# A routed expert stage: 256-slot tiles against 64 full tiles and seven half tiles

## Time and profile before

| what | value |
|---|---|
| median of three runs | 830.58 us |
| the profiled execution's own time | 830.82 us |
| its span, first to last instruction | 829.0 us |
| instructions | 17062 |
| TensorE busy | 798.3 us, 96% |
| VectorE busy | 508.3 us, 61% |
| ScalarE busy | 372.2 us, 45% |
| GpSimd busy | 438.5 us, 53% |
| moved by DMA | 93.35 MB |

### The profile page before, as it was taken

One profiled execution on the slowest core, in us unless ns is written; L12 is line 12 of the kernel. 1 busy time (PEld: TensorE's weight loads), 2 busy tenths in 40 slices (PEclk: granted clock), 3 DMA queues, 4 the chain that ended last, 5 costly groups with the idle time before them and its releaser, 6 DMA issues.

```text
span 829.0 us, 17062 instructions
## 1 busy us (share of the span) xinstructions
PE 798.3 (96%) x5609; PEld 716.9 (86%) x5609; DVE 508.3 (61%) x1081; ACT 372.2 (45%) x658; POOL 438.5 (53%) x345
## 2 busy tenths in 40 slices
PE   2999979999999999999999999999999999999997
PEld 1554449999999999999999999999999999998786
DVE  6878954565767666567656455456565655454586
ACT  3884143444545444445445444345454544443340
POOL 4632241665665765666665665665666666643100
PEclk9999999999999999999999999999999999999999
DMA  9989731333544433334434433334454343332895
GB/s 296 341 259 319 121 96 46 58 64 58 129 68 105 86 64 57 56 63 90 100 66 109 78 64 62 53 62 89 101 113 90 64 63 64 51 45 32 253 367 204
DMA packets 88206, 93.35 MB, mean 113 GB/s; under 512 B 15282, under 2 KB 79540, under 8 KB 88180
## 3 DMA queue, kind: packets, MB, share of 16 engines
q0 software_dynamic: 27264, 37.39, 27.6%
q1 hardware_dynamic: 51476, 55.32, 20.8%
q10 hardware_dynamic: 9440, 0.34, 1.0%
HBM read 48.66 MB, written 44.37 MB: 112 GB/s over the span
## 4 chain that ended last, share of the span: by engine, by line
PE 88%; DVE 8%; DMA 2%; issue 1%; ACT 1%; POOL 0%; POOLq 0%; DVEq 0%; SPq 0%
PE bank L1133 16%; PE bank L1132 16%; PE bank L1134 16%; PE bank L1162 16%; PE bank L1163 8%; PE bank L1206 5%; PE bank L1121 4%; PE bank L1034 3%; DVE xnT L797 2%; PE bank L998 2%; DVE stats L666 1%; PE bank L1010 1%; DVE xnT L809 1%; PE bank L1202 1%; DMA x_sb<-L_attn_x 1%
## 5 line engine op out<-in xcount | busy, mean ns | idle before, releaser
L424 POOL DMA_INDIRECT y_rows<-y_sb,token_idx x142 | 230.4, 1623 | 217.7 <-DVE y_sb L875 178.8
L1132 PE MATMUL bank<-xh,W_sb 128*128 128x256 f32 x1136 | 318.8, 281 | 3.1 <-DVE xl L852 3.1
L1133 PE MATMUL bank<-xh,W_sb 128*128 128x256 f32 x1136 | 319.3, 281 | 0.0
L1134 PE MATMUL bank<-xl,W_sb 128*128 128x256 f32 x1136 | 318.3, 280 | 0.0
L863 DVE TENSOR_TENSOR hbuf<-hbuf,bank 128x512 f32<-128x512 f32 x142 | 97.6, 687 | 216.8 <-PE bank L1134 216.8
L1132 PEld LDWEIGHTS bank<-xh,W_sb 128*128 128x128 f32 x1136 | 214.9, 189 | 6.7 <-issue 3.5
L1133 PEld LDWEIGHTS bank<-xh,W_sb 128*128 128x128 f32 x1136 | 214.6, 189 | 0.0
L1134 PEld LDWEIGHTS bank<-xl,W_sb 128*128 128x128 f32 x1136 | 213.7, 188 | 0.0
L1162 PE MATMUL bank<-W_sb,hh 128*128 128x512 f32 x568 | 209.4, 407 | 0.0
L415 POOL DMA_INDIRECT xg<-xn_rows,token_idx x142 | 165.6, 1166 | 67.4 <-issue 43.0
L1163 PE MATMUL bank<-W_sb,hl 128*128 128x256 f32 x568 | 159.6, 281 | 0.0
(11 more groups left out here) (157 smaller groups left out, 640.4 us busy)
## 6 DMA issues: line engine op xcount, KB each, us to landing
raw<-L_ffn_W SPq DMA_DIRECT2D x24, 512.0 KB, 4.0
x_sb<-L_attn_x SPq DMA_DIRECT2D x16, 512.0 KB, 6.8
xn_rows<-h_sb SPq DMA_DIRECT2D x16, 512.0 KB, 5.5
y_rows<-xnT SPq DMA_DIRECT2D x4, 2048.0 KB, 16.8
yy<-y_rows SPq DMA_DIRECT2D x16, 512.0 KB, 8.8
out<-x_sb SPq DMA_DIRECT2D x15, 512.0 KB, 7.5
xg<-xn_rows,token_idx POOLq DMA_INDIRECT x142, 3.0
y_rows<-y_sb,token_idx POOLq DMA_INDIRECT x142, 3.8
```

What stands on the lines that cost most here:

```text
L424: eng.indirect_dma_start(out=y_rows, out_offset=bass.IndirectOffsetOnAxis(ap=token_idx[:, 2 * i + t:2 * i + t + 1], axis=0), in_=y_sb[:, i ...
L1132: eng.matmul(part, high, x_h, start=k == 0, stop=False)
L1133: eng.matmul(part, low, x_h, start=False, stop=False)
L1134: last = eng.matmul(part, high, x_l, start=False, stop=k == KD - 1)
```

## The change

Slots are given out in halves of 128. An expert with h halves gets h // 2 pairs of halves, worked on as 256-slot tiles, and if h is odd one half left over. There are always 64 pair tiles (`PAIR_TILES`) in 8 groups of 8 steps (`GROUP`) and seven half tiles (`ODD_TILES`), one in each of the first seven groups. A last expert's odd half is taken into the pair tiles; pairs beyond 64 are spread over half tiles. Unused tiles work on unused slots. `token_idx` has 136 columns.

```diff
-EXP_TILES = 2 * T // TW + E - 1
-SLOT_TILES = EXP_TILES * TW // P
+PAIR_TILES = 2 * T // TW
+ODD_TILES = E - 1
+SLOT_TILES = 2 * PAIR_TILES + ODD_TILES + 1
+GROUP = 8
+LOADED_AGAIN = range(4, 16)
```

**Memory.** x is kept only for chunks 0 to 3 (`x_kept`). Chunks 4 to 15 (`x_late`) share their place with the half tile's own weights (`odd_raw`, `odd_W`) and buffers, and are loaded a second time after the last half tile's scatter:

```diff
+            eng.wait_ge(odd_stored, 16 * ODD_TILES)
+            for c in LOADED_AGAIN:
+                load_x(c)
```

```diff
+            eng.wait_ge(pairs_ready, 1)
+            def count(out, numbers, limits):
+                n = numbers.shape[1]
+                each = compared[:, 0:n * E].rearrange("p (n e) -> p n e", e=E)
+                link(eng.tensor_tensor(each, numbers..., limits..., ALU.subtract))
+                link(eng.tensor_scalar(each, each, 0.0, 1.0, ALU.max, ALU.min))
+                link(eng.tensor_tensor(each[:, :, 0:4], each[:, :, 0:4], each[:, :, 4:8], ALU.add))
+                link(eng.tensor_tensor(each[:, :, 0:2], each[:, :, 0:2], each[:, :, 2:4], ALU.add))
+                link(eng.tensor_tensor(out, each[:, :, 0], each[:, :, 1], ALU.add))
...
+            count(odds_until, plan_no[:, 1:EXT + 1], odd_from)
...
+            count(switches, plan_no[:, 0:PAIR_TILES + 1], first_at)
...
+            count(expert_at, plan_no[:, 0:E + 1], switch_of)
```

```diff
+            def gather(i):
+                column = planned(eng, COLUMN_AT + i, SLOT_TILES - 2)
+                link(eng.tensor_copy(token_at[:, 2 * i:2 * i + 2], token_idx[:, bass.ds(column, 2)]))
+                for t, rows in enumerate(tokens(i)):
+                    eng.indirect_dma_start(out=xg[:, i % XG_RING, t, :], ...)
...
+            for i in range(PAIR_TILES):
+                n, j = i % GROUP, i // GROUP
+                if i + XG_RING < PAIR_TILES:
                     wait_apart(eng, slot_weighed, i + 1)
                     gather(i + XG_RING)
+                if i == 0:
+                    odd_plan()
+                    eng.wait_ge(odd_plan_ready, 2)
+                    odd_gather(0)
+                if n == 5 and j + 1 < ODD_TILES:
+                    wait_apart(eng, odd_weighed, j + 1)
+                    odd_gather(j + 1)
                 scatter(i)
+                if n == GROUP - 1 and j < ODD_TILES:
+                    odd_scatter(j)
```

```diff
+            def load_next(n, switch):
+                e = planned(eng, PAIR_EXPERT_AT + switch, E - 1)
+                wait_apart(eng, w_low[n], switch)
+                load_w(eng, n, e).then_inc(raw_loaded[n], 16)
+            def high_if(switch, n):
+                with eng.If(switch > 0):
+                    eng.wait_ge(raw_loaded[n], switch * 16 + 16)
                     high(n)
+                    for m in ((), (0, 1), (2,))[n]:
+                        load_next(m, switch + 1)
```

**The half tile.** Its tokens are the stationary operand and its weights move. It uses one PSUM bank (6). On TensorE its pieces stand between the up product and the transposes of a step:

```diff
+            def odd_gate_up(j, half):
...
+                for n, w_at in enumerate((0, W3_AT)):
+                    part = ps_odd[:, n * D:(n + 1) * D]
+                    for k in range(KD):
...
+                        eng.matmul(part, x_h, high, start=k == 0, stop=False)
+                        eng.matmul(part, x_h, low, start=False, stop=False)
+                        last = eng.matmul(part, x_l, high, start=False, stop=k == KD - 1)
...
+            def odd_piece(n, j):
+                if n == 3:
+                    odd_transpose_x(j)        # 2 transposes
+                elif n in (4, 5):
+                    odd_gate_up(j, n - 4)     # 12 matmuls of 256 columns
+                elif n == 6:
+                    odd_transpose_h(j)        # 4 transposes
+                elif n == 7:
+                    odd_down(j)               # 4 of 512 columns, 4 of 256
+            def step(j, n, first=False, odd=True):
+                i = j * GROUP + n
+                gate(i + 1)
+                up(i + 1)
+                if odd:
+                    odd_piece(n, j)
+                transpose_x(...)
+                down(i, n % 2, first=first)
```

More of the change, by code:

```diff
@@ L187, in build @@
         chosen = tab[3][:, 0:TILES * E // 2].bitcast(bf16)
-        total, tiles_of, ends, starts, base = late(E), late(E), late(E), late(E), late(E)
+        ends, starts, base = late(E), late(E), late(E)
         total_i = late(E, i32)
@@ new lines, in _ @@
+            now, just_now = switches[:, 1:PAIR_TILES + 1], switches[:, 0:PAIR_TILES]
+            switched = plan_f[:, SWITCH_AT:SWITCH_AT + PAIR_TILES]
+            link(eng.tensor_tensor(switched, now, just_now, ALU.subtract))
+            link(eng.tensor_tensor(switched, switched, now, ALU.mult))
+            link(eng.memset(switch_of[:, 0:1], 0.0))
+            for e in range(1, E):
+                link(eng.tensor_tensor(switch_of[:, e:e + 1], switch_of[:, e - 1:e], active[:, e:e + 1], ALU.add))
@@ L598, in expert_step @@
                     keep_y_low(i - 1)
-                    high_if(e, 2)
+                    high_if(switch, 2)
+                if odd_ended is not None:
+                    odd_keep_y_low(odd_ended)
+                if odd is not None:
+                    odd_piece(n, odd)
                 if not gate:
                     return
-                for n in range(2):
-                    silu(i + 1, n)
+                for half in range(2):
+                    silu(i + 1, half)
                 if xT:
-                    high_if(e_next, 0)
+                    high_if(switch_next, 0)
                 h_high(i + 1, 1 - r, 0)
@@ L775, in _ @@
             link(eng.tensor_tensor(T2, T2, T3, ALU.mult))
+            link(eng.tensor_single_scalar(total_i, total_i, 1, ALU.logical_shift_right))
+            link(eng.tensor_copy(pairs, total_i))
+            eng.tensor_tensor_scan(pair_ends, ones[:, 0:E], pairs, 0.0, ALU.mult, ALU.add).then_inc(pairs_ready, 1)
             by_choice = slot.rearrange("p (j k) -> p j k", k=2)
@@ L884, in expert_step @@
                     add_y(i - 1, 1 - r, stored)
-                    low_if(next_expert(i), 2)
+                    low_if(switch_at(i), 2)
+                if odd_ended is not None:
+                    odd_add_y(odd_ended)
+                if odd is not None:
+                    odd_piece(n, odd)
                 if not gate:
@@ L897, in expert_step @@
                 if xT:
-                    low_if(e_next, 1)
+                    low_if(switch_next, 1)
                 h_low(i + 1, 1 - r, 1)
+                if odd is not None and n in (2, 3, 4):
+                    odd_low(odd, n - 2)
             for n in range(2):
@@ L905, in _ @@
             eng.wait_ge(choice_ready, 1)
+            eng.wait_ge(plan_ready, 3)
+            switch = switch_at(0)
+            for n in range(2):
+                low_if(switch, n)
             x_low(0, 0)
@@ L908, in _ @@
             low(2)
+            low_if(switch, 2)
             expert_step(-1, 3, w2=False)
```

474 lines of the change are left out of this document (346 added, 128 removed).

## The result

The changed kernel takes 821.98 us (median of four runs, 820.43 to 823.31) against 830.58 before (also four runs): ratio 0.9893, 95% interval 0.9872 to 0.9914. That is 8.6 us faster. The forecast was 808.8 us, 21.8 us faster. The range reached to 822 and just holds the time, but less than half of the forecast gain came.

The account below looks back on a forecast made before the run. TensorE was taken as the bound, busy 90.00 of 90.00 us in the expert stage. Tiles -28.1, head +3.5 and +0.8, steps +2 and tail zero sum to -21.8, giving 808.8 us; range 802 to 822.

Parts of the forecast that it names:

- the one on ScalarE's queue: Switch steps: ScalarE's load issues wait for VectorE's low part; last h_low ends at 215.0, TensorE wants it at 215.5; no cost.
- the rival of refetched loops: Longer loop bodies refetch code at some five back edges: +10 us by ScalarE, +20 on TensorE; within a 0.17 chance.
- the +2 that I had: Steps: extra half-tile conversions on VectorE meet switches prepared in steps 12, 26 and 50; +2 us (0 to 9).
- The head's term: Head: four parts delay or follow VectorE's start on the table, together +3.5 us.
- GpSimd beside it ... +2.6: Head: GpSimd's plan slows VectorE's one-hots by 0.18 us on some 14 batches, +2.6 us (0 to 14.6).
- +0.6 and -0.4: Head, VectorE: three more linked small operations, +0.6 us; 136 columns in place of 142 in 16 one-hots, -0.4 us.
- The rival of full serialization: Head: all 14.6 us of GpSimd work go to VectorE's chain in place of 2.6, +12, 821 us; chance 0.11.
- +0.7: Head: GpSimd's token step is ready later than VectorE's table wants it, +0.7 us (0 to 5).
- +0.8: Head: value load, copy and link on GpSimd in front of the first gather, +0.8 us (0.2 to 1.5).
- the forecast 123 to 125: Sign in the head: TensorE's first transposes come at 123 to 125 us instead of 119.85.
- the tiles: Expert stage: 7 of 71 tiles removed, 62.4 us; seven half tiles added, 34.3 us; net -28.1 us.
- GpSimd does not become the bound: Rival in the steps: gather extras exceed GpSimd's 2.61 us free per step; 863 us at 3.5 per gather; within 0.07.

Follow-up runs that it names:

- e11: e2 with the pair tiles' load code put back into ScalarE's loop, under a condition never true that the compiler keeps; 813.38 us.
- e1: The changed kernel with ScalarE's six groups after the first written out instead of looped, so no jump back on ScalarE; 811.77 us.
- e2: The changed kernel with the pair tiles' weights loaded by the SP queue again, the expert read from the plan; 808.92 us.
- e5: The changed kernel with the half tile's weight conversions cut to 8 of 1024 columns in groups 1 to 6; 820.68 us.
- e4: The changed kernel with GpSimd's plan filled with constants instead of computed, no switches of experts, output not the reference's; 803.58 us.
- e7: e2 with SP's loads held back until the first gathers have landed; 811.65 us.

## Why the prediction was wrong

**The step that failed** is the one on ScalarE's queue, where the reckoning ends with "So it fits, by half a microsecond" and the sum has nothing for it. Inside the step it did fit: of the seven steps that hold these issues six (7, 26, 31, 46, 50 and 53) lose about 0.1 us or less, and only step 12 loses more. But the jump back at the group's end was taken for free there; it stood only in the rival of refetched loops, at a low weight (within 0.17). The runs show that ScalarE's loop, grown from 2 steps to 8 and with the load code in every step, makes its engine idle for 3.1 to 4.5 us behind the jump back (e11: by the code's presence alone), and that where this meets a switch's load issues, TensorE pays (e1: written out, 7.5 of 9.8 us go; e2: loads elsewhere, all go). The middle of a group is near the +2 that I had: 0.99 us in step 12 and 1.15 in step 27. But the reason I gave, the half tile's conversions on VectorE, carries only step 12's share (e5), and both go with the loads (e2).

The Trainium skill ("Runtime: NRT & Kernel Launch", "Instruction fetch mechanics") has it that a taken branch out of the window of two pages stalls the engine until the page is there. ScalarE's rows agree, with 2.4 to 3.6 us between the branch and the next instruction and a packet of q14 in each gap. VectorE's first loop, which has the scan in it, waits 2.9 and 3.5 us at its two jumps, its second, without the scan, 0.3; TensorE loses nothing by it, in e2 either. TensorE's loop also grew to 8 steps and shows no such wait: in e2 it is busy 570.00 of 570.00 us.

**The rival of refetched loops** was the nearest: its place and the cover by ScalarE's free time were right. It spread the price evenly, 2 us at each of five jumps back. In fact the jumps ahead of steps 16, 24 and 40 cost nothing, and those ahead of 32 and 48 cost 7.2 together.

**The head's term was mis-sized.** "GpSimd beside it ... +2.6" is 6.0 us (e4). The other two terms, +0.6 and -0.4, fit together: e4 starts on the table at 110.75, before it was 110.69. I scaled from one row's slowdown, 1.34 to 1.45, beside operations on 71 elements, and spread it over 14 batches. In fact 4.7 of the 6.0 fall beside the two wide counts and nearly nothing beside the small links. The rival of full serialization (14.6) didn't come either.

Here the Trainium skill ("SBUF — State Buffer", "Who interferes with whom") and the rows agree in part. Its lock for a whole instruction is what 79.06 looks like, 1.03 us where e4 has 0.23, ending with GpSimd's; but that operation has one input, and for such the section has the lock only in the mode that uses both ports, which no row shows. The one-hots have two inputs in SBUF and should be shut out by any GpSimd instruction that reads SBUF; the pair at 91.64 was not (1.31 us, as alone, beside the 2.30 us from 90.47), as far as GpSimd's rough spans tell. By full locking the stretch would lose 14.6 us, and it lost 6.0; the measurement decides.

The token step was done at 108.65, not late: 0 in place of +0.7. From the table's start to the first gather's it takes 3.51 us instead of 1.98: value load, copy and link cost 1.5, nearly twice the +0.8. But from there to the first transposes it takes 4.85 instead of 7.18, in e4 too (8.3 from the table's start, here 8.36, before 9.16); of these 2.3 us the first gather operation itself gives 0.4 (1.73 instead of 2.17), and weight loads that are no longer beside the gather 1.2, by e7 against e2; 0.7 stay open. Before, SP issued two loads of 0.5 MB at 113.74 and 114.87, beside the gather (SP's timeline before; the third load is at 123.35):

```profile
113.74 9.98 SPq L326 DMA_DIRECT2D raw<-L_ffn_W  x3
```

In the changed kernel the DMA queues are idle from 114 to 122 and ScalarE's first load is issued at 124.77. So the change gave -0.8 in place of the +0.8 of the forecast, which had only looked at what GpSimd does. The first transposes, at 124.78, are inside the forecast 123 to 125 by errors of opposite sign.

**Not foreseen:** ScalarE's two load issues stand ahead of its first `x_high` (2.82 us of "issue" at 126.73), 1.2 us on the first product (3.41 us behind the first transposes, 2.23 before). Up to step 0 most of that is given back: in the 8 us behind the start of the first product the granted clock was 0.82, and 0.65 before. Step 0 is 5.15 us late.

**Right:** the tiles. From step 0 to step 61 the changed kernel took 589.2 us, less 9.8 of stalls 579.3; the forecast's arithmetic gives 61 x 8.916 + 34.3 = 578.2, and e2, which has no stalls, 578.5. In e2 half tiles' pieces wait for nothing; GpSimd does not become the bound; `odd_plan` (134.7 to 150.7) is hidden; the reload of x is, too.

**By size:** forecast -21.8; of the 11.5 us that the span missed (818.7 against 807.2), 7.8 are the stalls beyond 2, 0.8 the small delays beside them, 0.9 the head (5.15 against 4.3), 1.7 the tail's clock, and 0.3 the tiles. e2, which takes away the failed step, ran at 808.92, and the forecast was 808.8. That they are so near is luck: e2's head and the tail's clock cost some 3 us more than forecast, and the +2 for the steps was not used.

**Open:** why in e2 the jump back is free with a loop that is still 8 steps long, that is, from which length on it costs; how the loss of VectorE divides over GpSimd's kinds of operation; why some executions have the lower clock in the tail.

## What to carry to other kernels

When a loop body grows, look up the number of code packets per queue and the waits put down to "issue" at the first instruction behind the jump back, before you trust the slack of that engine. The packets alone don't tell: e1 has 60 of them and no such wait, since it doesn't jump. ScalarE's time to spare hid one such wait of up to 3.6 us here, but not one of 4.3, nor one that met another delay. Put seldom-run code, such as loads at a switch, on an engine whose queue is idle (SP here: 13 us), not under conditions inside the busiest loop. A slowdown between two engines read from a row with small operations doesn't hold for wide ones. And when an issue moves, look at what it ran beside: the loads that left the first gather's side gave back more than the new instructions ahead of it cost.

## What was not expected of the hardware

Code that is not run costs time: 34 packets more, and 3.9 to 4.5 us behind each jump back (e11 against e2). After an idle time of 2 us in the tail TensorE's granted clock was 1.00 in some executions and 0.66 in others of the same work, worth 1.7 us. GpSimd's arithmetic held VectorE up by up to a whole operation beside some wide ones (79.06), not beside the longest (91.64), and hardly beside those on one element.
